# Narrow attentions: values and ones in one stationary tile, and a batch's sums and values brought to their rows by 0/1 products

## What is computed

```
xn      = layernorm(x)                       # [8, 256, 128]
q, k, v = xn @ Wq.T + bq, ctx @ Wk.T + bk, ctx @ Wv.T + bv     # 16 heads of 8
w       = softmax(q k^T / sqrt(8) [+ bias, masked in layer 1])  # per batch and head, 256 x 256
x       = x + (w @ v) @ Wo.T + bo
```

## Time and profile before

| | |
|---|---|
| median of 3 runs | 1469.46 us |
| all three | 1465.37, 1477.18, 1469.46 us |
| the profiled execution | 1461.97 us, of which the span 1460.2 us |
| PE busy | 1318.7 us (90%) |
| DVE busy | 1039.4 us (71%) |
| ACT busy | 899.9 us (62%) |
| POOL busy | 913.2 us (63%) |
| `mix` (L757) on PE | 2048 records, 140.5 us |
| layer 1's narrow attention | about 747 to 993 us of the span |
| layer 3's narrow attention | about 1248 to 1431 us of the span |

### The profile page before, as it was taken

How to read it: one execution, slowest core, us unless ns; L and a number is a source line. 1 busy time by engine, 2 the same in 40 slices (tenths; PEclk the granted TensorE clock), 3 DMA queues, 4 the chain that set the end, 5 groups by cost and what they waited for, 6 DMA issues and landing times.

```text
span 1460.2 us, 37325 instructions
## 1 busy us (share of the span) xinstructions
PE 1318.7 (90%) x14582; PEld 807.8 (55%) x14582; DVE 1039.4 (71%) x2493; ACT 899.9 (62%) x1487; POOL 913.2 (63%) x879
## 2 busy tenths in 40 slices
PE   5999999997979999999979999986989799799987
PEld 3466566665757777777743433433567466344435
DVE  7888888888744344444647989986698477677775
ACT  4677787774859999999934544432234332465556
POOL 6788887876658999899857646522262120655535
PEclk9899999999989999999968999997989899799999
DMA  8000000000013110000101021000000000000000
GB/s 276 9 9 9 9 9 9 2 2 17 29 34 100 60 34 29 29 29 14 67 4 33 34 66 33 31 2 29 1 2 3 8 1 1 8 9 5 5 2 30
DMA packets 26083, 39.64 MB, mean 27 GB/s; under 512 B 7314, under 2 KB 13365, under 8 KB 25429
## 3 DMA queue, kind: packets, MB, share of 16 engines
q1 hardware_dynamic: 25364, 35.58, 7.5%
q0 software_dynamic: 576, 2.10, 0.7%
HBM read 38.72 MB, written 1.05 MB: 27 GB/s over the span
## 4 chain that ended last, share of the span: by engine, by line
PE 59%; DVE 25%; POOL 6%; issue 5%; ACT 4%; DMA 1%; SPq 0%; POOLq 0%; DVEq 0%; ACTq 0%
PE bank L1870 11%; PE bank L1811 10%; DVE sbuf L920 6%; PE bank L757 3%; PE bank L2336 2%; DVE sbuf L330 2%; PE bank L1264 2%; PE bank L709 2%; PE bank L1368 2%; PE bank L2094 2%; POOL sbuf L1216 2%; DVE sbuf L937 2%; PE bank L1296 2%; PE bank L1345 2%; PE bank L2315 2%
## 5 line engine op out<-in xcount | busy, mean ns | idle before, releaser
L1821 ACT ACTIVATE sbuf<-bank,sbuf 128x512 f32<-128x512 f32 (+1 forms) x512 | 323.1, 684 | 30.2 <-PE bank L1811 18.1
L1841 POOL TENSOR_TENSOR sbuf<-sbuf 128x512 f16<-128x512 f32 x256 | 304.9, 1199 | 56.4 <-ACT sbuf L1821 55.2
L1870 PEld LDWEIGHTS bank<-sbuf 128*128 128x128 f16 x3072 | 194.1, 98 | 67.4 <-issue 7.7
L1870 PE MATMUL bank<-sbuf 128*128 128x128 f16 x3072 | 214.4, 220 | 6.4 <-DVEq L1958 6.4
L310 POOL TENSOR_TENSOR sbuf<-sbuf 128x2 f32<-128x2 f32 (+1 forms) x48 | 39.7, 827 | 285.0 <-DVE sbuf L305 280.1
L1811 PE MATMUL bank<-sbuf 128*128 128x512 f16 x768 | 209.1, 382 | 0.0
L920 DVE TENSOR_REDUCE sbuf<-bank 128x4 f32<-128x1024 f32 x128 | 156.4, 1222 | 57.1 <-PE bank L709 42.2
L1953 DVE SCALAR_TENSOR_TENSOR sbuf<-bank,sbuf 128x128 f32<-128x128 f32 x256 | 71.7, 342 | 166.2 <-PE bank L1870 165.9
L1216 POOL TENSOR_TENSOR sbuf<-sbuf 128x512 f16<-128x512 f32 x128 | 147.9, 1176 | 57.1 <-ACT sbuf L1463 57.0
L757 PE MATMUL bank<-sbuf 128*32 128x256 f32 x2048 | 140.5, 394 | 1.6 <-ACT sbuf L857 1.6
L1210 POOL TENSOR_TENSOR sbuf<-sbuf 128x512 f16<-128x512 f32 x96 | 111.3, 1175 | 23.0 <-ACT sbuf L1451 22.9
(11 more groups left out here) (319 smaller groups left out, 2736.9 us busy)
## 6 DMA issues: line engine op xcount, KB each, us to landing
sbuf<-w SPq DMA_DIRECT2D x32, 256.0 KB, 2.9
sbuf<-bias_t SPq DMA_DIRECT2D x4, 1024.0 KB, 12.3
sbuf<-ctx_t SPq DMA_DIRECT2D x24, 128.0 KB, 2.4
sbuf<-bias_q POOLq DMA_DIRECT2D x4, 512.0 KB, 11.4
sbuf<-mask_t SPq DMA_DIRECT2D x8, 256.0 KB, 2.7
sbuf<-bias_t SPq DMA_DIRECT2D x8, 256.0 KB, 3.0
sbuf<-mask_q SPq DMA_DIRECT2D x8, 256.0 KB, 3.6
sbuf<-bias_q SPq DMA_DIRECT2D x8, 256.0 KB, 4.2
```

Of the source, the lines that this page charges most:

```text
L1821: last = act.activation(to, bank[u % 4][:, :], ACT.Gelu, bias=b1[u // U][:, u % FT0:u % FT0 + 1], scale=1 / SCALE)
L1841: g.tensor_tensor(hid16[1][:, u % BUFS, :], hid[:, u % 4, :], hid16[0][:, u % BUFS, :], ALU.subtract)\
L1870: last = pe.matmul(bank[4 + out_no % 2][:, j * P:(j + 1) * P], hid16[h][:, u % BUFS, j * P:(j + 1) * P], w2_16[p][:, w, f * D:(f + 1) * D] ...
```

## The change

- Zero and one columns: the values' stationary tile gets ones beside the values, 16 columns on. A window of 32 columns then gives values in 8 output rows and sums in 8 others. `window` shifts it by 8 for every second group, so that groups 0 and 1 fill the 32 rows of a head in the first half of the bank, and groups 2 and 3 those of the second half. `tens` is gone.
- `mix` is still called once a unit, but part m now handles key block m, with 4 products in place of 8: values and sums come out together.
- Since values and sums now stand in each other's way, a batch's bank is copied to SBUF by ACT (`take_out`, 128x512, unit 2 of the next batch, ahead of ACT's `project`), and PE brings sums and values to rows with four fp32 products of 128x128 by 128x256 with 0/1 matrices (`select`, unit 3, after `project`), into the same bank.
- DVE's `norm_out` moves from unit 2 to unit 3 and waits for `select`.
- The 0/1 matrices come as one more load of 256 KB among the weights; DVE sets the ones once per layer; a semaphore of POOL's mask work is folded into another with the same waits; retention's context comes in one DMA.

```diff
-                    for m in range(SB):
-                        for j in range(HG):
-                            at = g * HG * 32 + 32 * j
-                            lhs = tens[:, g, :] if part else val[b % 2][:, m, at:at + 32]
-                            at = (j % 2) * HW + m * S
-                            last = pe.matmul(bank[O_BANK[b % 2]][32 * j:32 * j + 32, part * S:part * S + S], lhs,
-                                             exps[:, (2 * Q + j // 2) % EXPS, at:at + S], start=g == part == m == 0,
-                                             stop=g == GROUPS - 1 and m == SB - 1, skip_group_check=True)
+                    m, to = part, bank[O_BANK[b % 2]][:, g // 2 * S:(g // 2 + 1) * S]
+                    for j in range(HG):
+                        lhs = val[b % 2][:, m, window(g, j):window(g, j) + 32]
+                        at = (j % 2) * HW + m * S
+                        last = pe.matmul(to[32 * j:32 * j + 32, :], lhs, exps[:, (2 * Q + j // 2) % EXPS, at:at + S],
+                                         start=g == m == 0, stop=g == GROUPS - 1 and m == SB - 1, skip_group_check=True)
                     last.then_inc(s["mixed"], 1)
+
+                def select(b):
+
+                    pe.wait_ge(s["taken"], b + 1)
+                    for k in (1, 0):
+                        for c in range(2):
+                            last = pe.matmul(bank[O_BANK[b % 2]][:, k * S:k * S + S], far["select"][:, 2 * k + c, :],
+                                             o_all[:, c * S:c * S + S], start=k == 1 and c == 0, stop=c == 1,
+                                             skip_group_check=True)
+                    last.then_inc(s["selected"], 1)
...
+                    if b and n == 3:
+                        select(b - 1)
...
+                def take_out(b):
+                    act.wait_ge(s["mixed"], 2 * GROUPS * (b + 1))
+                    wait(act, s["selected"], b)
+                    act.activation(o_all, bank[O_BANK[b % 2]], ACT.Copy).then_inc(s["taken"], 1)
...
+                    if b and n == 2:
+                        take_out(b - 1)
...
                 def norm_out(b):
-                    v.wait_ge(s["mixed"], 2 * GROUPS * (b + 1))
                     o = bank[O_BANK[b % 2]]
-                    v.reciprocal(rden, o[:, S:2 * S]).then_inc(s["rden"], 1)
-                    v.wait_ge(s["rden"], b + 1)
+                    v.wait_ge(s["selected"], b + 1)
+                    c.step(v.reciprocal(rden, o[:, S:2 * S])).settle()
...
-                    if b and n == 2:
+                    if b and n == 3:
                         norm_out(b - 1)
...
-            LOADS = 2
+            LOADS = 1
```

More of the change, by code:

```diff
@@ L90, in shape_constants @@
     at = np.broadcast_to(np.arange(EMAX, dtype=float), (P, EMAX))
+    select = np.stack([(p[:, None] == p[None, :] + 16 * (k - c)) & (row[None, :] // 16 == c)
+                       for k in range(2) for c in range(2)], 1).astype(float)
     return {
@@ L567, in narrow_attention @@
             att_t = take([S])
+            o_all = take([2 * S])
             if not masked:
@@ L588, in loads @@
                 if masked:
-                    wait(sp, s["masks"], 2 * b)
+                    wait(sp, s["masks"], made(b - 1, 1) if b else 0)
                     for k, name in enumerate(("t", "q")):
@@ L820, in tensor, with heads @@
                     mix(B * GROUPS - 1, part)
+                select(B - 1)
                 after.turn(pe, B - 2, B - 1, bank[TR])
                 out(B - 1)
+            def heads(b, t, at):
+                return val[b % 2][:, t, :].rearrange("p (g c) -> p g c", g=GROUPS)[:, :, at:at + HG * 32]\
+                    .rearrange("p g (j c) -> p g j c", c=32)
             def scalar(act):
@@ L886, in first, with made @@
                 v.tensor_scalar(bqs, bq, DH ** -0.5, None, ALU.mult).then_inc(s["ready"], 1)
-                c.step(v.memset(tens, 0.0)).settle()
-                for g in range(GROUPS):
-                    last = v.memset(tens[:, g, DH * g:DH * g + DH], 1.0)
-                v.memset(row16[0:1, 3, :], 1.0)
-                last.then_inc(s["ready"], 1)
+                v.memset(row16[0:1, 3, :], 1.0).then_inc(s["ready"], 1)
                 for p in range(2):
                     last = v.memset(val[p], 0.0)
+                c.step(last).settle()
+                for p in range(2):
+                    for t in range(SB):
+                        last = v.memset(heads(p, t, DH)[:, :, :, 16:16 + DH], 1.0)
                 last.then_inc(s["ready"], 1)
+            def made(b, k):
+                return 4 * b + 2 * k if b or k else 1
             def masks(v, b, k):
@@ L3069, in laid_out @@
         r[n] = c.astype(np.float32)
-    for n in ("at", "expert", "causal", "own", "block", "turn"):
+    for n in ("at", "expert", "causal", "own", "block", "turn", "select"):
         r[n] = r.pop("c_" + n)
```

33 lines of the change are left out of this document (18 added, 15 removed).

## The result

| | before | changed |
|---|---|---|
| median | 1469.33 us (4 runs) | 1538.57 us (4 runs) |
| all runs | 1465.37 to 1477.18 | 1537.25 to 1539.99 |
| ratio | | 1.0469, 95% interval 1.0429 to 1.0509 |
| span of the profiled execution | 1460.2 us | 1536.2 us |

The forecast was 1497 us with a range of 1464 to 1512. The direction held; the time is 42 us above the forecast and 27 us above the range.

The account below looks back on a forecast made before the run. The prediction held that PE and DVE wait for each other in turn, with norm_out's delay in DVE's queue deciding. Layer 1's +17.1 and layer 3's +10.8 gave +27.9 us: 1497 us as a median, range 1464 to 1512.

Parts of the forecast that it names:

- The direction: Whole kernel: slower, given a chance of 0.72, against 0.16 for same and 0.12 for faster.
- mix: PE in both attentions: half the products save 0.43 us a call, 1.00 to 0.57, with 64 calls in each layer.
- the fourth rival: PE's mix: weight loads or issue hold it at 1.00 us despite fewer products; +54 us, 1523; chance 0.06.
- select: PE, unit 3: four fp32 products priced from project cost 2.12 us a batch, 34 us for 16.
- DVE's queue: DVE, unit 3: norm_out waits about 2.4 us for select, delaying unit 4; batches about 30.9 and 23.4 us.
- the walk: Middle batches traced unit by unit through PE and DVE: +2.4 us each in layer 1, +1.6 in layer 3.
- the first rival: Both attentions: PE is the bound, so only products count; -21 us, 1448; chance 0.12.
- The first batches: First batch of each layer, without select: 3.0 us shorter in layer 1, 2.1 in layer 3.
- third rival: PE in the batches: waits drop its clock, some 5 us a batch, +20 us in four batches, 1517; chance 0.10.
- The two attentions with their ends: Layers 1 and 3: +17.1 and +10.8 us, together +27.9.
- the logits: Layer 1's last batch: select stands behind 2.85 us of gate logits on PE; the batch gets +2.6 us.
- The copy and its signals: Serial ends of both layers: ACT's take_out with its signals adds 0.7 us; inside batches costed at nothing.

Follow-up runs that it names:

- x1_filler: The changed kernel plus PE products that nobody reads, in unit 5 of every batch but a layer's first: 1509.90 us, ratio 1.0262.
- y1_no_select_filler: The changed kernel without take_out and select, plus unread PE products in unit 5 and in layer 1's unit 2: 1468.54 us, ratio 0.9985.
- y2_early_filler: The changed kernel with take_out in unit 1, select in unit 2, plus unread PE products in unit 5 and layer 1's unit 2: 1494.95 us.
- x2_no_select: The changed kernel without take_out and select, norm_out in unit 3 waiting for mix alone: 1491.57 us, ratio 1.0137.
- w2_before_pause: The kernel before plus an unread reciprocal of about 1.2 us in DVE's unit 4, ahead of cut, not in first batches: 1501.08 us, ratio 1.0217.
- z1_gap: The changed kernel with select in PE's unit 5, norm_out in DVE's unit 5, out in unit 6, addition to x in unit 7: 1505.65 us.
- y4_before_again: The kernel before, profiled once more with no edit: 1467.73 us, ratio 0.9977.
- w1_gap_more_filler: z1_gap plus unread PE products: layer 1 in unit 7 and ahead of unit 2's turn, layer 3 in units 6 and 7: 1501.00 us.
- x4_early: The changed kernel with take_out in ACT's unit 1 and select in PE's unit 2, norm_out left in unit 3: 1519.03 us, ratio 1.0332.

## Why the forecast missed

**The direction: right, and for its reason.** At full clock too a middle batch is longer than before (30.39 against 28.53 us, 22.57 against 21.80), so slower was no luck.

**mix: right.** Forecast 0.57 us a call, measured 0.57. A mix held up by weight loads or issue, the fourth rival, did not appear.

**select: right in kind, 0.29 us too dear.** Forecast 2.12, measured 1.83: eight records of one shape in a row run at 0.23 us each, where the pairs of project that priced them ran at 0.265.

**DVE's queue: the wait is there, its worth was too high.** Forecast a wait of about 2.4 us, measured 2.07 and 1.83. At full clock a middle batch is 30.39 and 22.57 us (x1_filler) where 30.9 and 23.4 were forecast: +1.9 and +0.8 us where the walk had +2.4 and +1.6. So the first rival, PE as the bound, falls: PE has only 25.96 us of work, fillers and all, in 30.39. The parts at full clock, in us a batch:

| | layer 1 | layer 3 |
|---|---|---|
| before (reciprocals at 886.25 and 914.78, 1350.84 and 1372.64) | 28.53 | 21.80 |
| mix halved, norm_out in unit 3 (y1_no_select_filler) | 28.06 | 20.72 |
| and take_out and select, in unit 2, DVE not waiting (y2_early_filler) | 29.78 | 22.02 |
| select in unit 3, DVE waiting: the change (x1_filler) | 30.39 | 22.57 |

Moving norm_out to unit 3 costs nothing that shows. Select costs 1.7 and 1.3 us without any wait of DVE, and its place in unit 3 with the wait 0.6 and 0.55 more. The walk put nearly all of it on the wait, so its sum was near for a reason that was in part another; why select costs so much of its 1.83 us where DVE does not wait was not taken apart. In layer 3 the walk had the halved mix give back 0.43 us a batch, and it gave 1.08.

**The first batches: nearly right.** From the layer's first reduction to the one in unit 2 of batch 1, 48.7 us before, 46.5 in the changed kernel and 45.4 in x1_filler in layer 1; 33.0, 34.7 and 31.7 in layer 3. Forecast were 3.0 and 2.1 us less; the falls of the clock hide it in the changed kernel.

**The clock: this is the step that failed.** The sum had it at nothing. The prediction had it as its third rival, at a chance of 0.10 and 20 us, with the sentence that PE "waits again only about 1 us at a stretch" and that the batches before kept 1.00 with DVE waits of 1.39 us. Three things were wrong in it. DVE's waits say nothing of PE's clock: it is PE's own idle time that counts, and the longest regular one in layer 3's units 3 to 5 had been 0.46 us. The 2.89 us of the earlier trace rows, the only fall that was looked at, were taken for the scale of what is needed, where 1.4 us can do (x2_no_select, w2_before_pause) and even 0.73 with a short one before it (z1_gap). And the "about 1 us" of PE's new wait stands without a working, though the walk had the numbers: in layer 3 select leaves PE 1.68 us late (1355.02 against 1353.34) and unit 4's mix gives back 0.43, while unit 4's reduction comes 2.6 us late. That adds 1.3 us to the 0.46, or 0.7 if the cut is 0.6 shorter; measured 1.68 in all. The size: the five middle periods of the changed kernel take 166.6 us in layer 1 and 125.9 in layer 3, where x1_filler has 154.4 and 112.5: 25.5 of the 31.9 us between the two spans; against full-clock periods throughout it is 15 and 13. That is 3 us for nearly every one of ten batches, not 5 us for four.

The Trainium skill (TensorE: Matmul & The Clock Gate, A second HAM failure mode) says that frequent short idle times between groups of matmuls make the clock go to and fro. The traces here agree: in the changed kernel it falls and comes back in nine of ten middle batches. The prediction named the rule and set it aside, because the batches before had idle times at full clock; they had shorter ones, place by place.

**The rest of the miss.** The two attentions with their ends were forecast at +27.9 us. With the clock mostly restored, x1_filler has 263.3 us for layer 1 (+22.6, forecast +17.1) and 188.9 for layer 3 (+9.4, forecast +10.8). What is left in layer 1 is in its last batches, where the clock is 0.74 even with fillers (37.17 us in the window above, 26.85 before). There select stands behind the gate's logits, and both ran at the lower level: the logits 5.29 us (L373, 987.16; 2.85 before) and select 3.76, while DVE stood 8.62 us ahead of the reciprocal. Costed were the logits at 2.85 and select at 2.12. In the changed kernel the logits took 3.97 us, and select came at the lower level in layer 1's last batch and at both ends, where layer 3's end had been costed at full clock:

```profile
1004.52 3.76 PE L774 MATMUL bank<-sbuf 128*128 128x256 f32 x8
...
1025.06 3.78 PE L774 MATMUL bank<-sbuf 128*128 128x256 f32 x8 [0.72 <-ACT sbuf L856]
...
1499.95 3.78 PE L774 MATMUL bank<-sbuf 128*128 128x256 f32 x8 [0.72 <-ACT sbuf L856]
```

The copy and its signals took 0.72 us there, as costed (0.7). Some 7 us of the difference of the two spans are not the change's (y4_before_again); the difference of the medians, 69 us, is free of that in part only, and how much the slower stretch between the layers weighs in each run was not measured.

**What stays open.** Why the last batches of both layers lose the clock more deeply than the middle ones was not taken apart; there PE has no project and waits more often, but no run changed only that. Nor does any run say which of two equal waits takes the clock, or why layer 3 lost it behind 0.73 us in z1_gap and kept it behind 1.01 in w1_gap_more_filler; the length of one wait does not decide alone.

**In sum.** The medians mix in the stretch between the layers (259.6 us in y2_early_filler, 268.7 in x1_filler, although nothing there differs), so the two attentions of the profiled executions are compared, in us:

| | layer 1 | layer 3 | both, against the row above |
|---|---|---|---|
| before | 240.7 | 179.5 | |
| mix halved, with fillers (y1_no_select_filler) | 241.2 | 174.0 | -5 |
| and select in unit 2 (y2_early_filler) | 256.3 | 189.3 | +30 |
| select in unit 3, DVE waiting (x1_filler) | 263.3 | 188.9 | +7 |
| without fillers: the changed kernel | 277.1 | 208.9 | +34 |

Of the 66 us, about half is clock that fillers give back, and most of the rest is select. Each row still holds some batches at the lower level, so the steps are good to a few us, and the +30 has clock in it too.

## What to carry to other kernels

Where PE and another engine take turns, work removed from PE turns into PE's idle time, so walk out the length of each wait of PE that the change makes or widens and compare it with the longest that the kernel has so far kept at full clock, place by place; here a wait that grew from 0.46 to 1.68 us was the warning, and in z1_gap, in another unit, 0.73 us was already too much. The runs give no length above which the clock falls each time or below which it never does: a wait that has grown is a risk, not a certainty. Price a fall by a whole batch with and without it (here 3 us of 22 to 30) and count it for every batch. Where two engines take turns, a piece put on one of them can cost nearly its full length though the other never waits for it (select, 1.3 to 1.7 us of 1.83). To tell clock from queues on the chip, put products that nobody reads into the wait: where the kernel gets faster with more work, it was the clock.

## What was not expected of the hardware

- The granted clock fell to 0.50 at waits of 1.41 to 1.68 us on PE, and not each time: waits of 1.41, 1.44, 1.56 and 1.68 us are each seen in a batch at 1.00 and in one at 0.80 or 0.81 (w2_before_pause, x4_early, w2_before_pause again, the changed kernel).
- It fell behind shorter waits too: 1.10 us in w2_before_pause (899.81), 0.98 in y1_no_select_filler (872.17), 0.73 with 0.22 shortly before it in z1_gap (1350.04). The kernel before kept 1.00 with 0.99 us in four middle periods of layer 1, w1_gap_more_filler with 1.01 and 1.11.
- In the changed kernel it fell from inside the wait (1367.39, in that of 1365.84 to 1367.51) to 2.1 us behind it (1343.50, behind the one that ended at 1341.35), and behind the waits of unit 5 it stayed at 0.50 for 7 to 14 us, with PE busy for 11.67 of 12 us at 846 to 858.
- Fillers in a wait cost nothing that shows and gave back 23 to 29 us (y1_no_select_filler, y2_early_filler, x1_filler).
- Two profiles of one program differ by 6.6 us in a stretch of 260 us (y4_before_again).
